# Softmax denominators in attention: step 8 joins VectorE's total, and TensorE sums the total first

## What is computed

```python
scores = jnp.einsum('bhqd,bhkd->bhqk', Q, K)
scores = jnp.clip(scores, -80.0, 80.0)
scores = jnp.where(causal, scores, -jnp.inf)
weights = jax.nn.softmax(scores / jnp.sqrt(jnp.float32(d_qk)), axis=-1)
attn = jnp.einsum('bhqk,bhkd->bhqd', weights, V)
```

## Time and profile before

| | us |
|---|---|
| median of 3 runs | 3002.51 (3002.14 to 3005.1) |
| the profiled execution | 3003.13 |
| its span, first to last instruction | 3001.4 |

### The profile page before, as it was taken

The page is one execution under the profiler, slowest core; times in us unless marked ns, Lnnn a source line. Parts: engine busy times, 40 slices in busy tenths (PEclk is TensorE's granted clock), DMA queues, the critical chain, the costliest instruction groups (busy, mean ns, idle before and its releaser), DMA issues.

```text
span 3001.4 us, 65378 instructions
## 1 busy us (share of the span) xinstructions
PE 2925.5 (97%) x22500; PEld 2134.2 (71%) x22500; DVE 2684.1 (89%) x4593; ACT 1589.5 (53%) x2330; POOL 580.7 (19%) x620
## 2 busy tenths in 40 slices
PE   7999899999999999969999999999999999999999
PEld 6777644444444444458888888888888888888887
DVE  7999788888888888869999999999999999999996
ACT  5666578778778778643333333333333333333333
POOL 3444300000000000012222222222222222222221
PEclk9999999999999999989999999999999999999999
DMA  7889956566566566441222222222222221221220
GB/s 241 283 288 301 285 126 148 131 147 143 133 150 137 137 151 135 130 127 54 58 60 60 60 60 59 51 58 58 59 60 60 59 59 54 56 58 57 59 57 30
DMA packets 335143, 333.27 MB, mean 111 GB/s; under 512 B 60368, under 2 KB 242512, under 8 KB 335056
## 3 DMA queue, kind: packets, MB, share of 16 engines
q1 hardware_dynamic: 335056, 332.26, 40.7%
HBM read 215.52 MB, written 116.65 MB: 111 GB/s over the span
## 4 chain that ended last, share of the span: by engine, by line
PE 56%; DVE 1%; ACT 0%; DMA 0%; POOL 0%; issue 0%; SPq 0%; DVEq 0%
PE p_ring L2010 21%; PE p_ring L2036 16%; PE ps_od L2010 12%; PE ps_od L1990 6%; PE p_ring L2024 1%; PE ps_od L2036 0%; PE p_ring L2052 0%; PE p_ring L2017 0%; DVE sb_wg_lo L1908 0%; PE p_ring L1990 0%; DMA sb_x<-in_L_attn_x_dram 0%; DVE sb_wd_lo L1908 0%; DMA dn<-sb_x_big 0%; DVE sb_x_amax L106 0%; DVE sb_x_big L118 0%
## 5 line engine op out<-in xcount | busy, mean ns | idle before, releaser
L1063 ACT ACTIVATE sb_probs<-scores 128x1024 f32<-128x1024 f32 (+3 forms) x512 | 405.8, 840 | 112.8 <-PE scores L1269 106.5
L1657 POOL TENSOR_TENSOR sb_stage<-sb_stage,sb_h_inv 128x512 f32<-128x512 f32 (+1 forms) x192 | 190.4, 992 | 866.6 <-DVE sb_h_inv L112 866.6
L2010 PE MATMUL p_ring<-sb_wg_hi,sb_xq_hi 128*128 128x512 f32 (+1 forms) x1024 | 294.8, 369 | 0.3 <-DVE sb_wd_lo L1908 0.3
L2010 PE MATMUL p_ring<-sb_wg_lo,sb_xq_hi 128*128 128x512 f32 (+1 forms) x1024 | 290.6, 365 | 0.0
L2010 PE MATMUL p_ring<-sb_wg_hi,sb_xq_lo 128*128 128x512 f32 (+1 forms) x1024 | 289.4, 363 | 0.0
L2036 PE MATMUL p_ring<-sb_wd_hi,sb_ht_hi 128*128 128x512 f32 x693 | 278.8, 402 | 0.0
L2036 PE MATMUL p_ring<-sb_wd_hi,sb_ht_lo 128*128 128x512 f32 x693 | 274.2, 396 | 0.0
L2036 PE MATMUL p_ring<-sb_wd_lo,sb_ht_hi 128*128 128x512 f32 x693 | 273.7, 395 | 0.0
L1269 PEld LDWEIGHTS scores<-sb_q_hi,sb_k_hi 32*128 32x128 f32 x1536 | 73.6, 182 | 280.7 <-ACT sb_probs L1063 156.6
L811 POOL TENSOR_TENSOR sb_at_in<-sb_at_in,sb_inv_in 128x512 f32<-128x512 f32 x64 | 95.0, 1484 | 910.4 <-DMA sb_inv_in<-dinv 910.1
L1727 ACT ACTIVATE sb_stage<-sb_stage,sb_code_zero 128x512 uint8<-128x512 f32 (+1 forms) x192 | 139.5, 727 | 241.8 <-DVE sb_stage L122 241.8
(11 more groups left out here) (215 smaller groups left out, 7202.4 us busy)
## 6 DMA issues: line engine op xcount, KB each, us to landing
kq<-sb_kq_out SPq DMA_DIRECT2D x32, 1024.0 KB, 7.2
sb_kq_raw<-kq SPq DMA_DIRECT2D x64, 512.0 KB, 6.9
sb_xin<-in_L_attn_x_dram SPq DMA_DIRECT2D x32, 512.0 KB, 6.9
v<-sb_v_out SPq DMA_DIRECT2D x64, 256.0 KB, 6.5
rq<-sb_r_out SPq DMA_DIRECT2D x64, 256.0 KB, 4.5
sb_qr<-rq SPq DMA_DIRECT2D x32, 512.0 KB
sb_kr_hi<-kr SPq DMA_DIRECT2D x32, 512.0 KB
sb_kr_lo<-kr SPq DMA_DIRECT2D x32, 512.0 KB
```

What stands on the lines that cost most here:

```text
L1063: act.activation(probs(k)[:, 2 * pair:2 * pair + 2, off:BANK], scores[(2 * k + pair) % RING2][:, :, off:BANK], ACT.Exp, scale=SCALE).then_ ...
L1657: pool.tensor_tensor(x, x, spread(h_inv[:, a // QB:b // QB], (b - a) // QB), ALU.mult).then_inc(h_y, 1)
L2010: i = pe.matmul(ps[:, m, 0:b0 - a0], xt[a][:, c, :], wg[b][:, m, c, a0:b0], start=(c == 0 and a == b == 0), stop=(c == DC - 1 and a == 1))
```

## The change

VectorE adds one more tile to the total: step 8's probabilities, in two new instructions a group (`add_fifth`), one for each pair of heads. `add_sums` of pair 1 moves from turn 10 to turn 9, where it follows that of pair 0; `add_fifth` of pair 0 is in turn 10 and that of pair 1 in turn 11, in odd groups ahead of the operations on the weights piece. TensorE no longer sums step 8 by itself (turn 9 has no denominator left), and step 9's denominator moves from turn 11 to turn 0'. Turn 0' now does TOTAL, 9, 10, 11, in that order, and TOTAL waits for four counts of the semaphore `total` instead of two. ScalarE's exponential of step 2' (which reuses step 8's tile) waits for the same four counts; before, it waited for step 8's denominator.

```diff
-DENOMS = [0, 1, 2, 3, 8, 9, 10, 11, TOTAL]
-DENOMS_AT = {3: [0], 4: [1], 5: [2], 6: [3], 9: [8], 11: [9]}
-DENOMS_NEXT = [10, 11, TOTAL]
+DENOMS = [0, 1, 2, 3, TOTAL, 9, 10, 11]
+DENOMS_AT = {3: [0], 4: [1], 5: [2], 6: [3]}
+FIFTH = 8
+DENOMS_NEXT = [TOTAL, 9, 10, 11]
@@
         def totals(it2, s):
 
-            return it2 * 4 + s * 2
+            return it2 * 8 + s * 4
@@
+                if k - PROBS + NS == FIFTH and not first:
+                    act.wait_ge(total, totals(*preceding(it2, s)) + 4)
@@
+            def add_fifth(it2, s, pair):
+
+                own(dve, total, totals(it2, s) + (pair + 1))
+                own(dve, clipped, step_no(it2, s, FIFTH) + 1)
+                heads = slice(2 * pair, 2 * pair + 2)
+                dve.tensor_tensor(added[:, 0, heads], added[:, 0, heads], probs(FIFTH)[:, heads],
+                                  ALU.add).then_inc(total, 1)
@@
                     elif k == 10 and s == 1:
-                        add_sums(it2, s, 1)
+                        add_fifth(it2, s, 0)
                         own(dve, w_rounded, rounded + 2)
@@
                     elif k == 9:
                         add_sums(it2, s, 0)
+                        add_sums(it2, s, 1)
                         if s == 1 and not (isinstance(it2, int) and it2 == 0):
@@
                     elif k == 10:
-                        add_sums(it2, s, 1)
+                        add_fifth(it2, s, 0)
                     elif k == 11 and s == 0:
+                        add_fifth(it2, s, 1)
                         own(dve, w_scaled, scaled + 4)
@@
                     elif k == 11:
+                        add_fifth(it2, s, 1)
                         own(dve, w_rounded, rounded + 3)
@@
                 if k == TOTAL:
-                    pe.wait_ge(total, totals(it2, s) + 2)
+                    pe.wait_ge(total, totals(it2, s) + 4)
```

## The result

The changed kernel takes 3217.32 us (median; 3215.12 to 3221.81) against 3003.81 us before: a ratio of 1.0713 with a 95% interval of 1.0694 to 1.0731, 213.5 us slower. The forecast was 3205, range 3140 to 3235. The profiled execution took 3221.81 us, its span 3220.1.

A forecast was written before the change was run, and what follows sets the result against it. TensorE looked the bound at 99.3% busy, but VectorE's queue has no pause in turns 9 to 11, so TensorE would stall for the total. 3003.1 + 143 (stalls) + 59 (half clock) = 3205 us, range 3140 to 3235.

The forecast's parts named there:

- stall at full clock, all boundaries: Turn 0': TensorE waits for VectorE's last add; 4.06 us lost per even boundary, 5.07 per odd, 143 in sum.
- half clock behind it: After each stall TensorE's clock falls to half: 0 to 2.4 us a group, taken as 1.9, 59 us over 31.
- VectorE's queue: Turns 9 to 0': VectorE runs without a gap, so the last add ends at 708.38 (odd) or 735.64 (even).
- TensorE's own gain: Step 8's matmuls removed from TensorE, 0.84 us a group, only lengthen its stall and are worth nothing.
- Place, not load: VectorE's load rises from 87% to 95% and fits on average; its free time lies in turns 1 to 4, not 9 to 11.
- Rival 1: Behind the stalls at turn 0' the clock holds or falls in few groups: 3146 to 3177 us; chance 0.20.
- rival 3: VectorE's adds stay hidden and step 8's matmuls on TensorE are saved, 27 us: 2976 us; chance 0.05.

The follow-up runs named there:

- e2: Changed kernel with 12 more matmuls of a constant, result overwritten, ahead of TensorE's wait for the total: 3148.58 us.
- e1: Changed kernel with 44 instead of 32 warm-up matmuls, putting TensorE's loop code where it lay before the change: 3213.55 us.
- e4: Kernel before plus VectorE's part alone: two more adds a group, read by nobody, add_sums 1 in turn 9; TensorE's work and order as before: 3065.21 us.
- e9: Changed kernel with TensorE's four half-1 sums and ScalarE's copy moved from turn 0' to turn 1', 44 warm-up matmuls: 3129.83 us.
- e7: Kernel before with TOTAL ahead of 10 and 11 in turn 0' and nothing else: 3004.84 us.
- e5: Changed kernel without the two new adds, step 8 left out of the denominators altogether: 3112.28 us.
- e8: Changed kernel without the two new adds, step 8 left out of the denominators, 44 instead of 32 warm-up matmuls: 3026.84 us.
- e11: Kernel before with 4 warm-up matmuls in place of 32 and nothing else: 3072.17 us.

## Why the prediction was right, point by point

**The sum.** The runs take it apart almost term by term. The measured column is a chain of differences from before to e2, e1 and the changed kernel, so it adds up by construction; its last term is hardly clear of noise.

| part | forecast | measured |
|---|---|---|
| stall at full clock, all boundaries | 143 | 145 (e2 less before) |
| half clock behind it | 59 | 65 (e1 less e2) |
| code loading | none | 4 (after less e1) |
| together | 202 | 214 |

**VectorE's queue.** Forecast without a gap from the first add to TOTAL: 6.76 us in the even group (728.93, where `add_sums` 0 stood, to 735.69); measured 6.75. This is why the stall came out to a tenth: 4.06 and 5.07 reckoned, 4.1 and 5.1 in e2. TensorE's own gain, the 0.84 us of step 8, was put at nothing, since it would only lengthen the wait. Right.

**Place, not load.** The reading of the earlier trace rows against the earlier trace rows holds: e4 has all of VectorE's new work and 61 of the 213 us; with the sums a turn later (e9) 84 us come back with the work unchanged. e7 shows that the order alone is innocent.

**The clock.** From two gaps in the trace of before I took 1.9 us a boundary; 65 us over 31 are 2.1. In the changed kernel it falls at all 31 boundaries, and e2 removes it. That the mean of two single gaps came so near is in part luck; what the rows gave was 1.4 to 2.4. The Trainium skill, "TensorE: Matmul & The Clock Gate", section "HAM oscillation — how this bites in real kernels", has a loop throttled anew in each turn in which TensorE pauses: the trace agrees. Its figure in "Part 1: The HAM clock gate", under 1% of a typical kernel's span for the ramp, does not carry over to a loop that pays at each of 31 boundaries: 65 us are 2.0% of this span. Rival 1 (3146, clock held) is what e2 is, at 3148.6.

**What was missed.** Code loading was in no term. It cost some 4 us here only because it fell into the stall; where there is none it cost 85 us (e5 less e8). The same miss shows in rival 3: I gave "the adds stay hidden" 2976 us, 27 saved. e8 gives the adds and step 8 away for nothing and takes 3027. The price of the removed matmuls was right and their worth was not: without them TensorE waits 0.20 us for a clip and 0.54 us for ScalarE ahead of turn 0', and 0.87 us for the clip of 11 in it (e8). Had VectorE been idle enough, the change would have been slower all the same, and I should have carried turns 9 to 0' through for that rival as I did for the forecast.

## What to carry to other kernels

An engine's free share says whether work fits, and the last idle bracket ahead of the place says whether it fits there: follow its queue back to that bracket, add the new work, and compare with the time at which the reader arrives. An in-order engine should meet a late operand last; whatever stands behind that wait, ready or not, is late by the same amount, and on TensorE a pause of 2 to 4 us was paid here a second time in clock. And where a small edit shifts code ahead of a long loop, look at the packets of the instruction queue before explaining a difference by the edit itself.

## What was not expected of the hardware

- Code of TensorE's loop was brought again in every turn (152 packets in place of 36) or not at all, depending on up to 28 matmuls ahead of the loop; a turn then waited 2.3 to 2.9 us at its start in e11 and 5.6 to 6.8 us in the changed kernel. Why the same number of packets costs so differently is not settled.
- The clock fell to 0.5 in e4 with no gap over 0.8 us near it, in a stretch with several short waits, in five of the loop's turns and not in the others, and in e9 behind a gap of 2.1 us. A gap of 3 us is not needed.
- Twelve useless matmuls a group made a kernel 65 us faster than the one without (e2 against e1), by holding the clock over a wait.
